# A graph layer in one kernel: SyncE's attention program written out, a bias row added by TensorE, block ends without GpSimd's drain

## What is computed

```python
xn = layernorm(x)
# graph attention, 4 heads of 64
xl, xr = xn @ W_l, xn @ W_r
e = leaky_relu(xl[src] + xr[dst], 0.2)
alpha = segment_softmax(einsum('ehd,hd->eh', e, att), dst)
gnn = layernorm(elu(segment_sum(alpha * xl[src], dst) + bias) + xn) * gamma + beta
# lambda layer: global context, no softmax over pairs
lam = batchnorm(softmax(xn @ W_k + b_k, axis=nodes).T @ (xn @ W_v + b_v))
mix = (xn @ W_q + b_q) @ lam
x = x + gnn + mix
# mixture of 8 experts, top 1, capacity 391
x = x + experts(layernorm(x))
```

## Time and profile before

| what | value |
|---|---|
| runs | 1646.53, 1651.84, 1654.27 us; median 1651.84 |
| profiled execution | 1640.94 us, its span 1639.2 us |
| instructions | 24931 |
| busy share of the span | PE 75%, PEld 53%, DVE 66%, ACT 52%, POOL 50% |
| mean granted PE clock | 0.875 |
| HBM traffic | 145 GB/s over the span |

### The profile page before, as it was taken

One profiled execution on the slowest core, in us unless ns is written; L12 is line 12 of the kernel. 1 busy time (PEld: TensorE's weight loads), 2 busy tenths in 40 slices (PEclk: granted clock), 3 DMA queues, 4 the chain that ended last, 5 costly groups with the idle time before them and its releaser, 6 DMA issues. The chain is left out here.

```text
span 1639.2 us, 24931 instructions
## 1 busy us (share of the span) xinstructions
PE 1232.8 (75%) x5659; PEld 869.4 (53%) x5659; DVE 1081.4 (66%) x2307; ACT 849.9 (52%) x3252; POOL 816.8 (50%) x849
## 2 busy tenths in 40 slices
PE   7848777767677776877787777777777757399995
PEld 5426555556455654655455555555565546355662
DVE  7546876768667775777667676677677859304444
ACT  3311465757566765666666566565665813132221
POOL 5615255655555655565555556555556264402213
PEclk9979898999799988898988989887898977599997
DMA  7545366556556665566566565565765125435340
GB/s 180 158 132 141 100 155 165 155 153 175 156 149 165 163 169 149 149 170 166 155 159 176 139 171 158 144 176 152 203 169 136 42 61 180 142 93 150 106 117 17
DMA packets 167497, 237.47 MB, mean 145 GB/s; under 512 B 40112, under 2 KB 134017, under 8 KB 167406
## 3 DMA queue, kind: packets, MB, share of 16 engines
q1 hardware_dynamic: 123310, 130.22, 27.9%
q0 software_dynamic: 41216, 103.67, 24.9%
q10 hardware_dynamic: 2880, 2.66, 0.5%
HBM read 189.57 MB, written 48.91 MB: 145 GB/s over the span
## 5 line engine op out<-in xcount | busy, mean ns | idle before, releaser
L1083 POOL DMA_INDIRECT gathered_rows<-d_xl,e_idx x576 | 546.9, 949 | 431.3 <-ACT e_prod L1512 201.8
L1512 ACT ACTIVATE e_prod<-gathered_rows,e_prod 128x64 f32<-128x64 f32 x2728 | 680.6, 335 | 53.0 <-issue 44.5
L1457 PE MATMUL bank<-e_prod,e_selt 128*128 128x260 f32 x1408 | 407.7, 433 | 120.7 <-DMA gathered_rows<-in_src_dram,n_row_of 43.1
L1457 PEld LDWEIGHTS bank<-e_prod,e_selt 128*128 128x128 f32 x1408 | 285.2, 211 | 218.3 <-issue 86.0
L1403 PE MATMUL bank<-e_xr,e_sel 128*128 128x256 bf16 x2112 | 329.8, 295 | 39.0 <-issue 24.2
L1157 DVE TENSOR_TENSOR e_edge<-bank,gathered_rows 128x512 f32<-128x512 f32 x176 | 119.8, 681 | 268.6 <-remote 236.7
L1403 PEld LDWEIGHTS bank<-e_xr,e_sel 128*128 128x128 bf16 x2112 | 219.5, 106 | 135.7 <-issue 60.1
L1408 PE MATMUL bank<-gathered_rows,ident 128*128 128x256 f32 x704 | 235.4, 415 | 39.6 <-issue 36.0
L1174 DVE TENSOR_REDUCE e_score<-e_edge 128x16 f32<-128x1024 f32 x176 | 212.9, 1210 | 0.3
L1408 PEld LDWEIGHTS bank<-gathered_rows,ident 128*128 128x128 f32 x704 | 118.9, 210 | 52.6 <-issue 41.3
L1508 ACT ACTIVATE e_prod<-e_diff 128x16 f32<-128x16 f32 x176 | 39.4, 224 | 205.3 <-remote 121.2
(11 more groups left out here) (315 smaller groups left out, 1130.5 us busy)
## 6 DMA issues: line engine op xcount, KB each, us to landing
e_xr<-d_xr SPq DMA_DIRECT2D x176, 192.0 KB
d_hist<-e_acc SPq DMA_DIRECT2D x176, 130.0 KB
e_drow<-d_rel SPq DMA_DIRECT2D x176, 128.0 KB
w_rows<-in_L_ffn_w_dram SPq DMA_DIRECT2D x16, 1024.0 KB, 7.3
gathered_rows<-d_xl,e_idx POOLq DMA_INDIRECT x576
d_in<-lambda_w SPq DMA_DIRECT2D x18, 350.7 KB
e_rows<-d_rows SPq DMA_DIRECT2D x22, 192.5 KB
x_rows<-in_x_dram SPq DMA_DIRECT2D x8, 512.0 KB, 4.8
```

The lines of the kernel that those rows point to most:

```text
L1083: pool.indirect_dma_start(xl[:, q.slot * G + g, :], None, m.d_xl, bass.IndirectOffsetOnAxis(ap=column, axis=0)).then_inc(gathered[q.slot], 16)
L1457: last = pe.matmul(ps_agg[b], selt[:, b, g, :], flat(prod[:, b, g, :, :]), start=(g == 0), stop=(g == G - 1))
L1512: last = act.activation(prod[:, b, g, h, 0:HEAD], xl[:, q.slot * G + g, h * HEAD:h * HEAD + HEAD], ACT.Copy, scale=prod[:, b, g, h, HEAD:H ...
```

## The change

1. SP's attention program is straight code for all 176 quads. One call loads four window starts each fourth quad, and without the check of their bounds. `drow` is loaded for two quads at a time (2 KB a partition, semaphore `numbered`), `xr` for each quad as before (`loaded`, now 16 each). `acc` is stored for two quads at a time. The other engines keep their loops.
2. `beta` joins `b_mix` by a third matmul in `mix_row`. In `mixes`, a matmul with one row of ones adds the `b_mix` row to each of 20 tiles. POOL's adds to `x` go, and SP waits for the reloaded `x`.
3. All four blocks are `nc.Block(no_gpsimd_drain=True)`: the engines meet by semaphores alone, and POOL doesn't run its drain at the end. 

```diff
+def window_bases(nc, m, sp, k):
+    return nc.values_load_multi_w_load_instructions(m.base[0:1, k:k + 4], engines=[sp.engine], min_val=0, max_val=LAST_BASE, ...)[1]
+def load_numbers(sp, m, k):
+    h = k // 2 % 2
+    numbers = m.d_rel[k * G:(k + 2) * G, :].rearrange("g e -> (g e)")
+    sp.dma_start(m.drow[:, 2 * h:2 * h + 2, :]..., numbers.partition_broadcast(P)).then_inc(m.numbered[h], 16)
+def load_window(sp, m, k, base):
+    sp.dma_start(m.xr[:, k % 4, :], m.d_xr[bass.ds(base * SPAN, P), :]).then_inc(m.loaded[k % 4], 16)
...
-    with nc.Block() as block:
+    with nc.Block(no_gpsimd_drain=True) as block:
...
+            bases = window_bases(nc, m, sp, 0)
             for k in range(4):
-                base = sp.value_load(m.base[0:1, k:k + 1], min_val=0, max_val=LAST_BASE)
-                sp.dma_start(m.drow[:, k, :], ...).then_inc(m.loaded[k], 16)
-                sp.dma_start(m.xr[:, k, :], ...).then_inc(m.loaded[k], 16)
+                if k % 2 == 0:
+                    load_numbers(sp, m, k)
+                load_window(sp, m, k, bases[k])
...
+            def load(k):
+                if k % 2 == 0:
+                    sp.wait_ge(s["sel"], k - 2)
+                    sp.wait_ge(s["edges"], k - 3)
                     settle(sp, m)
+                    load_numbers(sp, m, k)
+                else:
+                    sp.wait_ge(s["edges"], k - 3)
                     settle(sp, m)
+                load_window(sp, m, k, bases[k % 4])
+            def store(k):
+                h = k // 2 % 2
+                sp.wait_ge(s["acc"], k + 2)
                 settle(sp, m)
+                sp.dma_start(m.d_hist[k * P:(k + 2) * P, :]..., acc[:, 2 * h:2 * h + 2, :, :]...).then_inc(stored[h], 16)
+            for k in range(QUADS + STORE_LAG):
+                if k < QUADS:
+                    if k >= 4:
+                        if k % 4 == 0:
+                            bases = window_bases(nc, m, sp, k)
+                        load(k)
...
+                if k % 2 == 1 and k > STORE_LAG:
+                    store(k - STORE_LAG - 1)
+            sp.wait_ge(sl["x"], 16 * (FOURS + 1))
...
-            pool.wait_ge(sl["mix"], 2)
-            pool.tensor_tensor(m.b_mix[:, :], m.b_mix[:, :], m.beta[:, :], ALU.add).then_inc(sl["rowed"], 1)
-            pool.wait_ge(sl["rowed"], 1)
-            pool.wait_ge(sl["x"], 16 * (FOURS + 1))
-            for b in range(FOURS):
-                four = m.x[:, 4 * b:4 * b + 4, :]
-                pool.tensor_tensor(four, four, m.b_mix[:, :].unsqueeze(1).to_broadcast([P, 4, DIM]), ALU.add)
...
-                dve.wait_ge(loaded[r], (q.of(4) + 1) * 32)
+                dve.wait_ge(numbered[r // 2], (q.of(4) + 1) * 16)
...
-                    dve.wait_ge(stored[r], q.of(4) * 16)
+                    dve.wait_ge(stored[r // 2], q.of(4) * 16)
...
+                last = pe.matmul(ps_wide[:, 0:DIM], m.ones[0:1, :], m.beta[0:1, :], start=False, stop=True)
...
-                pe.wait_ge(loaded[r], (q.of(4) + 1) * 32)
+                pe.wait_ge(loaded[r], (q.of(4) + 1) * 16)
...
+                    pe.matmul(mix(n), m.ones[0:1, :], m.b_mix[0:1, :], start=False, stop=False)
                     pe.matmul(mix(n), m.ident[:, :], m.x[:, n, :], start=False, stop=True).then_inc(s["mixps"], 1)
```

More of the change, by code:

```diff
@@ L198, in shared_memory @@
     m.used = [0, 0]
+def window_bases(nc, m, sp, k):
+    return nc.values_load_multi_w_load_instructions(m.base[0:1, k:k + 4], engines=[sp.engine], min_val=0, max_val=LAST_BASE,
+                                                    skip_runtime_bounds_check_because="the table is clipped to this range where it is made")[1]
+def load_numbers(sp, m, k):
+    h = k // 2 % 2
+    numbers = m.d_rel[k * G:(k + 2) * G, :].rearrange("g e -> (g e)")
+    sp.dma_start(m.drow[:, 2 * h:2 * h + 2, :].rearrange("p q e -> p (q e)"), numbers.partition_broadcast(P)).then_inc(m.numbered[h], 16)
+def load_window(sp, m, k, base):
+    sp.dma_start(m.xr[:, k % 4, :], m.d_xr[bass.ds(base * SPAN, P), :]).then_inc(m.loaded[k % 4], 16)
 def ring_view(m, half, partitions, *shape, dt=F32):
@@ L942, in attend @@
     s = sem_set(nc, m.sems, "att", "init idx sel edges summed relu score lin turned run top ends heads fwd bwd carried drop cols raised tops topped diff rr f fac ex prod selt agg old acc rows* links fixed shares")
-    sl = sem_set(nc, m.sems, "lam", "chain less e ctxps ctx wqps wq turnedps turned lamps lam var rstd bn mixps mix rowed x clear")
-    loaded, gathered = m.loaded, m.gathered
-    stored = [m.sems.enter_context(nc.semaphore(f"att_stored{r}")) for r in range(4)]
+    sl = sem_set(nc, m.sems, "lam", "chain less e ctxps ctx wqps wq turnedps turned lamps lam var rstd bn mixps mix x clear")
+    loaded, numbered, gathered = m.loaded, m.numbered, m.gathered
+    stored = [m.sems.enter_context(nc.semaphore(f"att_stored{h}")) for h in range(2)]
     idx = [sb(f"e_idx{q}", [P, SUBS_RUN], I32) for q in range(2)]
@@ L1002, in spread_link @@
         return row.unsqueeze(1).to_broadcast([1, HEADS, SUBS_RUN])
-    with nc.Block() as block:
+    with nc.Block(no_gpsimd_drain=True) as block:
         @block.sync
         def _(sp):
[L1007 to L1012, removed]
-                    settle(sp, m)
[L1014 to L1022, removed]
-                    settle(sp, m)
[L1024 to L1029, removed]
```

42 lines of the change are left out of this document (21 added, 21 removed).

## The result

The changed kernel takes 1679.38 us (median of four executions, 1657.02 to 1679.85) against 1652.22, a ratio of 1.0143 with a 95% interval of 1.0091 to 1.0196. I had forecast 1646.6 us and a range up to 1661. It is slower, by 1.4%, and outside of the range. (Two single ones of over 2600 us are left out of the means.)

What follows compares the result with a forecast made beforehand. Attention was taken as bound by a PE-DVE chain with gathers, no single engine. Terms -5 -1.4 -0.8 +0.6 +5.9 -3.4 -1.1 = -5.2 us, carried to the median, gave 1646.6 us; 8-in-10 range 1628 to 1661.

Steps and rivals of the forecast that it cites:

- the term of PE's rows: Node update: one-row matmuls for 20 tiles, 0.43 us a tile at full clock, 0.9 at half; +5.9 us, bounds +2 and +8.
- rival B: Node update: the rows on PE are free, by full clock or hidden by DVE; 0 for +5.9, 1640.8 us; chance 0.11.
- Attention: Attention stage: SP's instructions off the path, paired drow loads send fewer packets; -5 us, between -19 and +17.
- rival A: Attention: gets quicker through lighter DMA work; -19 us instead of -5, 1632.6 us; chance 0.20.
- rival C: Attention: SP's paired transfers hold up gathers, 0.8 us 22 times; +17 instead of -5, 1668.6 us; chance 0.14.
- my own sign: Attention: the prediction counts as wrong if this stage moves by more than 10 us either way.
- The ends of blocks: Last two blocks: POOL's drains go, -3.4 us after the node update's scatters and -1.1 us at the experts' end.
- Rival D: Block ends: another wait takes the drain's place, so 4.5 us of drains stay; 1651.1 us; chance 0.05.
- The survey's end: End of the survey, SP last: two drow issues and four bounds checks go; -1.4 us, bounds -1.1 and -1.9.
- GpSimd's adds: End of attention: POOL's five adds to x go, which had slowed one DVE select from 344 to 1143 ns; -0.8 us.
- Rival E: End of attention: POOL's adds to x blocked DVE throughout; 11.7 us gained instead of 0.8, 1635.7 us; chance 0.04.
- the 204 us: Attention, 126 quads: DVE's idle time before the edge add, 204.3 us; shares of PE and DMA left open.

Runs made afterwards that it cites:

- experiment 6: Changed kernel with the b_mix row's matmul fed by 128 rows of weights (b_mix divided by 128) instead of one: medians 1646.63 and 1648.16 us.
- experiment 7: Changed kernel with the one-row matmul done twice in a row, each with half of b_mix: median 1662.19 us, ratio 1.0076.
- experiment 1: Kernel before with SP's new program alone, drains and POOL's adds to x kept: median 1648.41 us, ratio 0.9988.
- experiment 4: Changed kernel without the row on PE; POOL adds to x as before, with a semaphore wait: median 1653.87 us, ratio 0.9997.
- experiment 11: Kernel before without drains, with the 128-row matmul on PE instead of POOL's adds, SP's program old: median 1647.28 us, ratio 0.9949.
- experiment 9: Changed kernel with SP's straight code, but drow loaded and acc stored for one quad at a time: median 1663.14 us.
- experiment 2: Kernel before without POOL's drains in the four blocks, last add to x waited for by semaphore: medians 1643.27 and 1647.07 us.
- experiment 10: Kernel before without the gathers of quads 16 to 175, the first 16 quads' rows read again: median 1322.26 us, ratio 0.8029.

## Why the prediction was wrong

**Direction and size: the term of PE's rows was mis-sized.** I took +5.9 us. The step that failed is "I count two passes more per tile, since each of the tile's three matmuls stands as two in the trace: 0.43 us a tile at full clock, 0.9 at half". It measured 0.81 and 1.31. The passes were right, as experiment 6 shows to the hundredth; what was missing is 0.39 us for the change of form, which experiment 7 isolates. The path and the cover were right too: in the 128-row form, at the price that I had put down, the node update without drain was 110.3 us where the one without any row was 107.6, so +2.7, inside of my +2 to +8. The nearest row of the trace had the form itself, one row of weights, at 0.63 to 0.79 us each, and I set it aside as alone and cold. It was the better one to take for the upper bound: with 0.79 us for each of the 12 tiles that are not covered it gives +9.5 us, over my bound of +8.

**The clock adds to it.** With 12 tiles at 0.81 to 1.31 us the delay of `places(0)` is 10 to 16 us; 13.4 was seen. In the later profiles PE was also at the half clock for longer: granted 0.59 and 0.57 over the block, 0.66 before and 0.68 in the first profile after, and a tile takes 4.01 us there and 2.11 at full speed. I had kept the clock's pattern of the first profile for the sum, with two tiles of four at the half clock. That the clock's pattern moves when the work before it gets longer was rival B's idea with the wrong sign: it did not stay full. Why the chip grants the half clock in one execution and not in another, these runs don't tell. Nor do they tell whether the rest of the change has a part in it: with the row alone the two node updates were 118.4 and 122.9 us with a drain in them, with all of it 120.0 to 134.5 without.

**Attention: no term, but scatter.** I took -5 us, between -19 and +17. `drow`'s packets fell as worked out, and nothing came of it: SyncE's new program makes -1.6, +7.0 or +4.3 us, each with an error of 3 to 4 (experiments 1, 4 and 11), and going back to single transfers changed nothing (experiment 9). Rivals A and C are both out by the size that I gave them. C's own sum was also off: beside the -0.2 of the other terms it decides from 8.5 us, 0.39 a run, and not from 13.5 and 0.6, in which the -5 was still counted. By my own sign (attention moving by more than 10 us) the first profile said that I was wrong there; the sign was too narrow, for the changed kernel's attention lies between 1200.4 and 1237.9 us by itself. What I should have seen is that the term's own uncertainty was not the range's main part. I had three times before me, 1646.5 to 1654.3, and took half a per cent for what a measurement can tell. 143 executions span 43 us, and a median of four of them is uncertain by some 5 or 6 us. Of the first measurement, +27 us, about half, 14, is the change's.

**The ends of blocks** were about right. The node update without its drain and without the row is 107.6 to 109.2 us against 109.9, 113.2 and 110.2, forecast -3.4; the experts 209.0 to 210.4 against 210.2 to 211.7, forecast -1.1. The drain of the survey and that of attention were hidden, as said. Rival D is out: no other wait took the drain's place.

**The survey's end.** From the first `drow` issue to the end of the last `xr` issue it was 111.52 + 0.35 - 106.44 = 5.4 us. After, the issues on SP, with their durations:

```profile
106.57 0.33 SPq L212 DMA_DIRECT2D e_drow<-d_rel  x1
107.12 0.90 SPq L217 DMA_DIRECT2D e_xr<-d_xr  x2
108.07 0.43 SPq L212 DMA_DIRECT2D e_drow<-d_rel  x1
108.69 0.86 SPq L217 DMA_DIRECT2D e_xr<-d_xr  x2
```

That is 108.69 + 0.86 - 106.57 = 3.0 us, so 2.4 less; forecast 1.4. It is lost in the block's own scatter: the surveys of these kernels took 104.0 to 116.2 us.

**GpSimd's adds.** Without them the longest `select` took 575 ns where it had taken 1143: the blocked instruction is gone, and that is 0.6 us of the 0.8. The lock that I weighed from the Trainium skill ("SBUF — State Buffer", Who interferes with whom) may be what that row showed. Rival E's 11.7 us are not there: the kernels that keep the adds (experiments 2 and 4) are no slower than those without.

**The chance.** I gave 0.14 to slower, all of it for rival C. The place where it went wrong had no rival at all: none ended on the slow side by PE's rows, though that was the one part that adds work to an engine without idle time. The Trainium skill ("TensorE: Matmul & The Clock Gate", Why this matters for your kernels) says that a single matmul with 32 rows takes the time of one with 128. By experiments 6 and 7 this holds here for a one-row matmul behind another (0.44 us, where one with 128 rows takes 0.42), and not between full ones (0.81).

## What to carry to other kernels

A one-row matmul in a row of full ones is priced by its change of form as well as by its passes: here 0.39 us on top of 0.43. Where the operand is already on all partitions, feeding it through all 128 rows of weights (and dividing it by 128) saved those 0.39 us a tile and the kernel 14. Before a difference of a per cent is explained, the same kernel should be profiled twice, block by block: the experts repeat within 3 us and can be argued on, the node update moves by 3 to 13 with the clock, and the attention, by 38 in the changed kernel, needs a mean over many executions. The lowest mean is that of the kernel before without the drains (experiment 2), 5.1 ± 2.7 us or 0.3% below it.

## What the runs showed beside

Attention's length scatters from execution to execution. In 17 profiles with gathers, of eleven programs, it lay between 1199.3 and 1246.0 us, while the experts lay between 209.0 and 211.7. The times in which no engine begins anything make up 132 to 181 us of it, and go with its length (correlation 0.84 over the 17). One such time in the kernel before, in order of time (start, length, engine, line):

```profile
833.28 1.77 ACT L1512 ACTIVATE e_prod<-gathered_rows,e_prod 128x64 f32<-128x64 f32 x6
833.35 1.15 PE L1403 MATMUL bank<-e_xr,e_sel 128*128 128x256 bf16 x9
...
834.99 0.95 POOL L1083 DMA_INDIRECT gathered_rows<-d_xl,e_idx  x1 [0.30 <-issue]
836.11 0.35 ACT L1512 ACTIVATE e_prod<-gathered_rows,e_prod 128x64 f32<-128x64 f32 x1 [1.06 <-issue]
836.12 0.27 PE L1403 MATMUL bank<-e_xr,e_sel 128*128 128x256 bf16 x1 [0.97 <-issue]
836.15 0.19 PEld L1408 LDWEIGHTS bank<-gathered_rows,ident 128*128 128x128 f32 x1 [1.17 <-issue]
836.82 0.35 ACT L1512 ACTIVATE e_prod<-gathered_rows,e_prod 128x64 f32<-128x64 f32 x1 [0.36 <-issue]
837.61 0.95 POOL L1083 DMA_INDIRECT gathered_rows<-d_xl,e_idx  x1 [1.67 <-DMA gathered_rows<-in_src_dram,n_row_of]
...
837.81 0.35 ACT L1512 ACTIVATE e_prod<-gathered_rows,e_prod 128x64 f32<-128x64 f32 x1 [0.64 <-issue]
```

ACT had begun one every 0.29 us (six in 1.77) and PE one every 0.13 (nine in 1.15). From 834.99 to 837.61 each begins one in 0.7 to 1.7 us, and the trace puts no releaser to it ("issue"). Experiment 10 shows that this comes with the gathers, whether from their DMA traffic or from GpSimd's issuing of them. Late gathers are not what the edge add waits for. In the trace of before the last of a quad's four gathers starts 12 to 23 us (median 15.8) ahead of its edge add, and this pair, around the rows above, shows more:

```profile
831.01 0.60 PE L1408 MATMUL bank<-gathered_rows,ident 128*128 128x256 f32 x2
...
842.21 0.69 DVE L1157 TENSOR_TENSOR e_edge<-bank,gathered_rows 128x512 f32<-128x512 f32 x1 [9.29 <-remote]
```

The matmuls at 831.01 are PE's last for this quad, and they stand behind PE's own wait for the same gathers, so these had landed. DVE's add, the next in its order, begins 10.6 us after they ended (by the end that the trace models for them). Counted over quads 35 to 159, 201 of 205 us of idle time before this add fall on quads whose last PE matmul had ended over 1 us earlier. That answers in part what the prediction left open about the 204 us: it is neither PE's matmuls nor a gather's landing, and what delays the signal between PE and DVE the trace doesn't name. Which resource the engines share with the gathers stays open too; I didn't try smaller gathers, or fewer of them with the same bytes. What goes with the gathers is the largest thing in this kernel: 330 us, of which the stretches without a start are 126.
